# Every second scan step takes its product with B from ScalarE and a transpose on TensorE, not from VectorE or GpSimd

## The chip, the cores and the metric

The kernel runs on one core of one Trainium2 chip. The metric is the device time of one execution in microseconds. Five engines work side by side, each through its own instructions in order: TensorE (PE, with its weight loads as PEld), VectorE (DVE), ScalarE (ACT), GpSimd (POOL) and SyncE (SP), which here only starts DMAs. Semaphores order the engines among each other.

## The reference, cut to what matters

The reference adds four blocks one after the other to an image batch of 8 x 32 x 32 x 64: a diffusion stage, a 3x3 convolution, a Mamba block and a two-dimensional DCT, each behind a group norm. The change is in the Mamba block's selective scan. Per image there are L = 1024 pixels in sequence, 128 inner channels and 16 states:

```python
def step(h, inp):
    u_t, d_t, B_t, C_t = inp
    dA = jnp.exp(d_t[..., None] * A)
    h = dA * h + (d_t * u_t)[..., None] * B_t[:, None, :]
    y = jnp.einsum('bdn,bn->bd', h, C_t)
    return (h, y)
...
return ys.transpose(1, 0, 2) + u * D
```

Here `d_t * u_t` is delta*u. It depends on channel and pixel; B and C depend on state and pixel, and are the same for all channels.

## The kernel before, in words

The 8 images are four pairs, and two pairs make a half; the kernel goes through all stages for half 0 and then for half 1 (`h`). A half has four images `j` in its scan phase, and a scan step `s` of 0 to 63 is one state of one image: `j = s // 16`, state `s % 16`. The layout in the scan is 128 channels on the partitions and 1024 pixels along the free dimension, so the scan over the pixels is one VectorE instruction.

One step needs, in this order:

- ScalarE, `decay` (L881): exp(delta * A) into the buffer `DA[s % 2]`. It waits for scan `s - 2`.
- The product delta*u*B. In three of four steps TensorE copies the row of B to all partitions by two bf16 matmuls with a selecting matrix (`b_rows`, L530; the row is kept as three bf16 parts that add up) into `PS[s % 2]` in PSUM, after scan `s - 2`, and VectorE multiplies it by delta*u in place (L1410). In every fourth step (`s % 4 == 3`, `by_pool`) a DMA copies the row from DRAM to all partitions (`b_row`, L243) and GpSimd multiplies (`input_times_b`, L321) into `DBP`; `decay` then writes its result to `PS[s % 2]`.
- VectorE, `scan_step` (L1403): the scan instruction (L1416) into `HS[s % 2]`. It waits for the decay, the product, and GpSimd's product of step `s - 2`, which reads the same `HS`.
- GpSimd, `state_times_c` (L314): the states times the row of C (L319), which a DMA has brought to all partitions (`c_row`, four buffers in turn), into `HC[s % 2]`. It waits for TensorE's sum of step `s - 2`.
- TensorE, `sum_of` (L538): adds that product to `PS[3]`, by matmuls with the identity; in the first step of an image the product with D is added too (L549). After an image's 16 steps VectorE's `gate` (L1418) reads the sum.

TensorE's order is written out in its loop (L689 to L736): in turn `s` first the broadcast for step `s + 2`, then the sum of step `s - 1`, and behind them the jobs of other stages: the next half's `x_channels` and `group_mean`, and, for the pair finished first, `skip`, `out_proj`, the norm, the last projection and the two DCTs (`xn2_channels` to `second_dct`). ScalarE's loop (L1085) has the decay of step `s` and behind it the copies and sums that belong to these jobs (`keep_x_sums`, `ln_of`, `last_scale`, `x3_sums`, `scale` and others). GpSimd's loop is at L405, VectorE's at L1534, and the queue of SP at L276. In all of them an instruction that waits holds up all behind it.

B and C come out of a projection in the 96 + 32 rows of a PSUM tile; ScalarE keeps the fp32 rows (`keep_rows`, L891) in unused partitions of `BCS32` and `R1`, from where `store_rows` (L226) brings them to DRAM for the row DMAs.

## Time and profile before

| | us |
|---|---|
| median of three runs | 1072.91 |
| lowest, highest | 1071.75, 1073.18 |
| the profiled execution's own time | 1076.65 |
| its span, first to last instruction | 1074.6 |

Busy time over the span: TensorE 824.9 us (77%), VectorE 871.7 (81%), ScalarE 440.2 (41%), GpSimd 656.0 (61%). Busy time does not count waits, and a matmul's duration contains the time in which it drains while the next one already runs; so starts of instructions that follow each other are closer than their durations say. The mean granted TensorE clock was 0.902 of the full 2.4 GHz. The scan phases are from about 276 to 510 us and from about 787 to 1019 us of the span.

### The profile page before, as it was taken

How to read it: one execution, taken by the hardware profiler on the slowest of the kernel's cores; microseconds unless marked ns; L12 is line 12 of the kernel's file. 1: busy time of each engine (PE TensorE's matmuls, PEld its weight loads, DVE VectorE, ACT ScalarE, POOL GpSimd, SP SyncE). 2: the span in 40 equal slices, each digit the busy share in tenths (PEclk: the TensorE clock that was granted, in tenths of full speed). 3: DMA queues.
4: the chain of work that ended last, by engine and by line, in shares of the span. 5: the costliest groups of instructions: out<-in, count | busy, mean ns of one | idle time of the engine just before them, and what ended most of it. 6: DMA issues, size and time to landing. Idle time of an engine off the chain costs nothing.

```text
span 1074.6 us, 6964 instructions
## 1 busy us (share of the span) xinstructions
PE 824.9 (77%) x2210; PEld 379.4 (35%) x2210; DVE 871.7 (81%) x672; ACT 440.2 (41%) x501; POOL 656.0 (61%) x294
## 2 busy tenths in 40 slices
PE   3977998976387877789885999897637787778835
PEld 2433443432133423244443444343213242334414
DVE  5999885479988999999897488547998899999830
ACT  3734331158545333455364423214843423345212
POOL 2446993111699797888361499311169979889810
PEclk8987999988689999999997999998968899999966
DMA  3000000003445564555000100000224555555401
GB/s 96 1 0 0 0 0 1 0 5 107 103 147 192 179 207 176 178 184 167 1 0 3 17 0 0 1 0 5 93 79 138 194 190 195 182 191 193 145 0 20
DMA packets 37808, 91.05 MB, mean 85 GB/s; under 512 B 16264, under 2 KB 16400, under 8 KB 37776
## 3 DMA queue, kind: packets, MB, share of 16 engines
q1 hardware_dynamic: 37456, 89.62, 25.2%
q0 software_dynamic: 320, 1.05, 0.4%
q8 instruction: 15, 0.25, 0.1%
q14 instruction: 17, 0.14, 0.1%
HBM read 87.51 MB, written 3.15 MB: 84 GB/s over the span
## 4 chain that ended last, share of the span: by engine, by line
DVE 39%; PE 32%; POOL 14%; issue 9%; ACT 5%; DMA 1%; SPq 0%; POOLq 0%; DVEq 0%; ACTq 0%
DVE arena L1416 10%; POOL arena L319 9%; PE ps L650 9%; PE ps L446 7%; DVE ps L1410 5%; PE ps L545 4%; ACT arena L754 4%; DVE arena L1371 3%; PE ps L644 3%; DVE arena L1273 3%; POOL arena L327 2%; PE ps L452 2%; POOL arena L312 1%; PE ps L591 1%; PE ps L435 1%
## 5 line engine op out<-in xcount | busy, mean ns | idle before, releaser
L319 POOL TENSOR_TENSOR arena<-arena 128x1024 f32<-128x1024 f32 x128 | 302.5, 2376 | 66.9 <-DVE arena L1416 40.1
L545 PE MATMUL ps<-arena,mat 128*128 128x512 f32 x512 | 270.2, 654 | 69.4 <-POOL arena L319 58.0
L1416 DVE TENSOR_TENSOR_SCAN arena<-arena,ps 128x1024 f32<-128x1024 f32 x96 | 219.5, 2287 | 20.1 <-POOL arena L319 17.2
L754 ACT ACTIVATE arena<-arena,Amat 128x1024 f32<-128x1024 f32 x96 | 109.9, 1148 | 170.6 <-DVE arena L1416 149.3
L545 PEld LDWEIGHTS ps<-arena,mat 128*128 128x128 f32 x512 | 100.6, 205 | 185.0 <-POOL arena L319 98.3
L754 ACT ACTIVATE arena<-arena 128x1024 f32<-128x1024 f32 (+4 forms) x124 | 80.7, 689 | 134.8 <-DVE arena L1339 74.8
L1410 DVE TENSOR_TENSOR ps<-arena,ps 128x1024 f32<-128x1024 f32 x96 | 116.2, 1210 | 4.8 <-PE ps L535 2.7
L650 PE MATMUL ps<-arena,mat 128*128 128x512 f32 x240 | 106.3, 592 | 0.0
L535 PE MATMUL ps<-arena,sel 96*128 96x512 bf16 x192 | 62.2, 409 | 54.5 <-DVE arena L1416 54.1
L446 PE MATMUL ps<-arena,diag 128*128 128x512 f32 x192 | 87.3, 614 | 2.1 <-ACT arena L754 2.1
L327 POOL TENSOR_TENSOR arena<-arena,BB 128x1024 f32<-128x1024 f32 x32 | 75.3, 2354 | 0.0
L754 ACT ACTIVATE arena<-ps 128x1024 f32<-128x1024 f32 (+2 forms) x52 | 52.8, 1017 | 54.2 <-DVE ps L1230 17.0
L1416 DVE TENSOR_TENSOR_SCAN arena<-ps,arena 128x1024 f32<-128x1024 f32 x32 | 72.8, 2276 | 0.2
L446 PE MATMUL ps<-arena,convw 128*128 128x512 f32 x144 | 67.0, 622 | 6.7 <-ACT arena L754 6.7
L650 PEld LDWEIGHTS ps<-arena,mat 128*128 128x128 f32 x240 | 45.6, 190 | 57.4 <-issue 57.4
L342 POOL TENSOR_TENSOR arena<-arena 128x1024 f32<-128x1024 f32 x8 | 24.8, 3108 | 65.7 <-DMA out<-arena 28.1
L754 ACT ACTIVATE ps<-arena,Amat 128x1024 f32<-128x1024 f32 x32 | 35.8, 1118 | 69.9 <-DVE arena L1416 65.2
L302 POOL TENSOR_TENSOR dr<-dv,cpow 128x16 f32<-128x16 f32 x8 | 23.9, 2986 | 58.0 <-DVE dv L1238 43.2
L298 POOL TENSOR_TENSOR dgn<-dgn,cpow 128x1 f32<-128x1 f32 x12 | 7.3, 610 | 83.7 <-DVE dgn L1197 66.7
L308 POOL TENSOR_TENSOR arena<-arena 128x1024 f32<-128x1024 f32 x8 | 21.6, 2704 | 60.0 <-DVE arena L1396 60.0
L535 PEld LDWEIGHTS ps<-arena,sel 96*128 96x128 bf16 x192 | 15.8, 103 | 115.6 <-DVE arena L1416 99.4
L446 PEld LDWEIGHTS ps<-arena,diag 128*128 128x128 f32 x192 | 37.4, 197 | 48.6 <-issue 46.4
(167 smaller groups left out, 1331.5 us busy)
## 6 DMA issues: line engine op xcount, KB each, us to landing
arena<-bc_rows SPq DMA_DIRECT2D x128, 512.0 KB, 4.1
BB<-bc_rows SPq DMA_DIRECT2D x32, 512.0 KB, 4.9
out<-arena SPq DMA_DIRECT2D x32, 64.0 KB, 2.2
xres<-x POOLq DMA_DIRECT2D x4, 256.0 KB, 5.2
bc_rows<-arena SPq DMA_DIRECT2D x8, 128.0 KB, 2.0
xres<-x SPq DMA_DIRECT2D x4, 256.0 KB, 4.4
convw<-conv_w SPq DMA_DIRECT2D x1, 576.0 KB
mat<-mats SPq DMA_DIRECT2D x1, 448.0 KB, 3.5
```

What stands on the lines that cost most here:

```text
L319: tt(HC[s % 2], HS[s % 2], CB[s % 4], ALU.mult).then_inc(S("hc"), 1)
L327: tt(DBP, two_images(s // D_STATE, "DU"), BB, ALU.mult).then_inc(S("dbp"), 1)
L446: last = mm(half(ps, n), taps(tap), frame[:, dy + HB * n:dy + HB * n + HB, dx:dx + W], start=(tap == first), stop=(tap == 8))
L535: last = mm(half(PS[s % 2], n), blk(sel, s % D_STATE), half(two_images(s // D_STATE, "BCS"), n)[0:96, :], start=True, stop=True)
L545: last = mm(half(PS[3], n), ident, half(HC[s % 2], n), start=first, stop=True, skip_group_check=True)
L644: last = mm(half(mix, n), ident, half(a["g"], n), start=False, stop=False, skip_group_check=True)
L650: last = mm(half(mix, n), mt(mname), half(a[src], n), start=False, stop=(name == "e"), skip_group_check=True)
L754: return nc.scalar.activation(out_, in_, func, bias=bias, scale=scale, accum_out=accum_out)
L1273: stt(t, frm(A[k]["fz"])[:, 0:H, tap:tap + W], vecs[:, col:col + 1], t, ALU.mult, ALU.add).then_inc(S("a_tap"), 1)
L1371: stt(d["XI"][:, t:L], PS[2 * k][:, 0:L - t], w[3 - t], d["XI"][:, t:L], ALU.mult, ALU.add)\
L1410: tt(PS[q][:, :], two_images(j, "DU"), PS[q][:, :], ALU.mult).then_inc(S("dbu"), 1)
L1416: nc.vector.tensor_tensor_scan(HS[q], a, b, 0.0, ALU.mult, ALU.add).then_inc(S("scan"), 1)
```

## The change

From step 9 on, every odd step (`X_STEPS`, 28 of a half) makes its product with B another way. Delta*u of the image, 128 channels by 1024 pixels, is turned once by TensorE into eight blocks with 128 pixels on the partitions (`turn_du`), and ScalarE keeps the turned blocks (`keep_du`). The 128 rows of B and C of the four images, now together in the tile `ROWS`, are turned once too (`turn_rows`), and ScalarE keeps B of it (`keep_b`). In this layout B of one state and block is one number per partition. So for step `s` ScalarE makes eight activations of 128x128, each a block times its scale (`scaled_input`, three steps ahead, two buffers `TB`), and TensorE turns the eight results back into `PS[s % 2]` (`turn_scaled`). VectorE scans this directly. All other steps (`Z_STEPS`, 36 of a half: 0 to 8 and the even ones) are made as three of four were before: broadcast by TensorE, product by VectorE. GpSimd's products with B, the row DMAs for them and the buffers `BB` and `DBP` go; `decay` always writes to `DA`.

The turned images pass through `PS[2]`, so TensorE's other jobs that use it are placed anew: `x_channels` and `group_mean` of the next half two turns later each, `skip(0)` from turn 21 to 32, `out_proj(0)` from 22 to 33. ScalarE's and GpSimd's parts of the next half's first norm move by two turns with them. Left out below: three semaphores of the setup and of the norms that are merged with others, and the call of `b_row` ahead of the loop.

```diff
@@ -112,9 +112,10 @@
             d = D[k]
-            d["BCS32"] = d["BCS"]
             d["BCS"] = d["BCS"].bitcast(bf16)
+            d["HI32"] = d["HI"]
             d["HI"] = d["HI"].bitcast(bf16)
+            d["END"] = arena[:, sum(n for _, n in later):][:, 0:BANK]
...
@@ -129,7 +130,9 @@
         DA, HS = [[D[0][f"W{2 * m + q}"] for q in range(2)] for m in (0, 2)]
-        DBP, BB = D[0]["R1"], sb("BB", L)[:, :]
+        ROWS = sb("ROWS", L)[:, :]
+        TB = [ROWS, D[1]["R1"]]
+        BT = D[0]["HI32"].rearrange("p (k j n) -> p k j n", k=BLK, n=D_STATE)
         CB = [D[0]["W2"], D[0]["W3"], D[1]["W0"], D[1]["W1"]]
...
@@ -153,16 +156,21 @@
         SCANS = 4 * D_STATE
-        BY_POOL = SCANS // 4
-
-        def by_pool(s):
-            return s % 4 == 3
-
-        def row_fill(s):
-            return s - s // 4 + 1
+        X_STEPS = [s for s in range(9, SCANS, 2)]
+        Z_STEPS = [s for s in range(SCANS) if s not in X_STEPS]
         def rows_f32(j):
-            return D[j // 2]["R1" if j % 2 else "BCS32"][96:128, :]
+            return ROWS[32 * j:32 * j + 32, :]
+
+        def du_block(j, n):
+            if j % 2 == 0:
+                return blk(D[1]["W4"], n)
+            return blk(D[n // 4]["END"], n % 4)
+
+        def turned(h, j):
+            return 5 * h + [1, 3, 4, 5][j]
+
+        ROWS_TURNED = 2
...
@@ -240,14 +248,6 @@
-            def b_row(h, s):
-                j = s // D_STATE
-                if s % D_STATE < 4:
-                    sp.wait_ge(S(f"rows{j % 2}"), 32 * h + 16 * (j // 2 + 1))
-                if s >= 4:
-                    sp.wait_ge(S("dbp"), BY_POOL * h + s // 4)
-                load_row(BB, j, s % D_STATE, "b_row")
-
             def store_out(h, k):
...
@@ -275,8 +274,6 @@
                     c_row(h, s)
-                    if s % 4 == 0:
-                        b_row(h, s + 3)
                     if s == SCANS - 3:
...
@@ -317,14 +314,6 @@
                 tt(HC[s % 2], HS[s % 2], CB[s % 4], ALU.mult).then_inc(S("hc"), 1)
-
-            def input_times_b(h, s):
-                pool.wait_ge(S("b_row"), 16 * (BY_POOL * h + s // 4 + 1))
-                if s % D_STATE == 3 and s > 3:
-                    pool.wait_ge(S("du"), 4 * h + s // D_STATE + 1)
-                if s >= 4:
-                    pool.wait_ge(S("scan"), SCANS * h + s - 3)
-                tt(DBP, two_images(s // D_STATE, "DU"), BB, ALU.mult).then_inc(S("dbp"), 1)
...
@@ -396,21 +385,13 @@
                 delta_u(h, 1)
-                pool.wait_ge(S("r10"), 2 * h + 2)
-                pool.wait_ge(S("bcs0"), ONE + 2 * h + 2)
-                plain(pool)
-                pool.wait_ge(S("rows1"), 32 * h + 16)
-                pool.wait_ge(S("du"), 4 * h + 1)
-                input_times_b(h, 3)
                 for s in range(SCANS):
                     state_times_c(h, s)
-                    if by_pool(s) and s + 4 < SCANS:
-                        input_times_b(h, s + 4)
                     if s == 5:
                         delta_u(h, 2 + s // 16)
-                    if h + 1 < HALVES and s in (13, 21):
+                    if h + 1 < HALVES and s in (15, 23):
                         root(A[s // 16], h + 1, 0, s // 16)
...
@@ -528,12 +509,31 @@
             def b_rows(h, s):
-                if s < SCANS and not by_pool(s):
-                    if s >= 2:
-                        pe.wait_ge(S("scan"), SCANS * h + s - 1)
-                    for n in range(2):
-                        last = mm(half(PS[s % 2], n), blk(sel, s % D_STATE), half(two_images(s // D_STATE, "BCS"), n)[0:96, :], start=True, stop=True)
-                    last.then_inc(S("bb"), 1)
+                if s >= 2:
+                    pe.wait_ge(S("scan"), SCANS * h + s - 1)
+                for n in range(2):
+                    last = mm(half(PS[s % 2], n), blk(sel, s % D_STATE), half(two_images(s // D_STATE, "BCS"), n)[0:96, :], start=True, stop=True)
+                last.then_inc(S("bb"), 1)
+
+            def turn_scaled(h, s):
+                i = X_STEPS.index(s)
+                pe.wait_ge(S("scaled"), len(X_STEPS) * h + i + 1)
+                pe.wait_ge(S("scan"), SCANS * h + s - 1)
+                transposes(TB[i % 2], PS[s % 2]).then_inc(S("bb"), 1)
+
+            def fill(h, s):
+                if s in Z_STEPS:
+                    b_rows(h, s)
+                if s in X_STEPS:
+                    turn_scaled(h, s)
+
+            def turn_du(h, j):
+                pe.wait_ge(S("du"), 4 * h + j + 1)
+                transposes(two_images(j, "DU"), PS[2]).then_inc(S("turned"), 1)
+
+            def turn_rows(h):
+                pe.wait_ge(S("kept"), turned(h, 0))
+                transposes(ROWS, PS[2]).then_inc(S("turned"), 1)
...
@@ -690,28 +690,41 @@
                         plain(pe)
-                    b_rows(h, s + 2)
+                    fill(h, s + 2)
                     sum_of(h, s - 1)
+                    if s == 2:
+                        pe.wait_ge(S("rx1"), 2 * h + 2)
+                        turn_du(h, 0)
+                    if s == 3:
+                        turn_rows(h)
+                    if s == 5:
+                        pe.wait_ge(S("kept"), 5 * h + ROWS_TURNED)
+                        turn_du(h, 1)
+                    if s == 23:
+                        if h + 1 < HALVES:
+                            pe.wait_ge(S("group1"), g_var(h + 1, 0))
+                        else:
+                            pe.wait_ge(S("kept"), turned(h, 1))
+                        turn_du(h, 2)
+                    if s == 28:
+                        pe.wait_ge(S("kept"), turned(h, 2))
+                        turn_du(h, 3)
+                    if s == 32:
+                        pe.wait_ge(S("kept"), turned(h, 3))
+                        skip(0)
                     if h + 1 < HALVES:
-                        if s == 5:
-                            pe.wait_ge(S("rx1"), 2 * h + 2)
+                        if s == 7:
+                            pe.wait_ge(S("kept"), turned(h, 1))
                             x_channels(h + 1, 0, PS[2])
-                        if s == 10:
+                        if s == 12:
                             group_mean(A[0], h + 1, 0, 0)
-                        if s == 13:
+                        if s == 15:
                             pe.wait_ge(S("a_x"), 2 * h + 3)
                             x_channels(h + 1, 1, PS[2])
-                        if s == 18:
+                        if s == 20:
                             group_mean(A[1], h + 1, 0, 1)
-                        if s == 21:
-                            pe.wait_ge(S("a_x"), 2 * h + 4)
-                            pe.wait_ge(S("group1"), g_var(h + 1, 0))
-                            skip(0)
-                    elif s == 21:
-                        pe.wait_ge(S("rx1"), 2 * h + 2)
-                        skip(0)
-                    if s == 22:
+                    if s == 33:
                         out_proj(h, 0)
...
@@ -881,12 +894,47 @@
                     j, q = s // D_STATE, s % 2
-                    act.wait_ge(S("delta"), 4 * h + j + 1)
+                    if s % D_STATE == 0:
+                        act.wait_ge(S("delta"), 4 * h + j + 1)
                     if s >= 2:
                         act.wait_ge(S("scan"), SCANS * h + s - 1)
-                    plain(act)
-                    dst = PS[q][:, :] if by_pool(s) else DA[q]
-                    av(dst, two_images(j, "DL"), ACT.Exp, Amat[:, s % D_STATE:s % D_STATE + 1]).then_inc(S("da"), 1)
+                    if s % D_STATE == 0:
+                        plain(act)
+                    av(DA[q], two_images(j, "DL"), ACT.Exp, Amat[:, s % D_STATE:s % D_STATE + 1]).then_inc(S("da"), 1)
+
+            def keep_du(h, j):
+                act.wait_ge(S("turned"), turned(h, j))
+                if j >= 2:
+                    act.wait_ge(S("scaled"), len(X_STEPS) * h + sum(1 for s in X_STEPS if s < D_STATE * (j - 1)))
+                if j == 0:
+                    act.wait_ge(S("delta"), 4 * h + 3)
+                    av(D[1]["W4"], PS[2][:, :], ACT.Identity).then_inc(S("kept"), 1)
+                elif j == 2:
+                    av(D[1]["W4"], PS[2][:, :], ACT.Identity).then_inc(S("kept"), 1)
+                else:
+                    av(D[0]["END"], half(PS[2], 0), ACT.Identity)
+                    av(D[1]["END"], half(PS[2], 1), ACT.Identity).then_inc(S("kept"), 1)
+
+            def keep_b(h):
+                act.wait_ge(S("turned"), 5 * h + ROWS_TURNED)
+                act.wait_ge(S("bcs0"), ONE + 2 * h + 2)
+                ps = PS[2][:, :].rearrange("p (k j n) -> p k j n", k=BLK, n=2 * D_STATE)
+                av(BT, ps[:, :, :, 0:D_STATE], ACT.Identity).then_inc(S("kept"), 1)
+
+            def scaled_input(h, s):
+                i, j = X_STEPS.index(s), s // D_STATE
+                if i == 0:
+                    for r in range(2):
+                        act.wait_ge(S(f"rows{r}"), 32 * h + 32)
+                if i == 1:
+                    act.wait_ge(S("bcs1"), ONE + 4 * h + 4)
+                if i > 1:
+                    act.wait_ge(S("bb"), SCANS * h + X_STEPS[i - 2] + 1)
+                if i == 0 or X_STEPS[i - 1] // D_STATE < j:
+                    act.wait_ge(S("kept"), turned(h, j) if i else 5 * h + ROWS_TURNED)
+                for n in range(BLK):
+                    last = av(blk(TB[i % 2], n), du_block(j, n), ACT.Identity, BT[:, n, j, s % D_STATE:s % D_STATE + 1])
+                last.then_inc(S("scaled"), 1)
...
@@ -1086,15 +1134,26 @@
                         hi_rows(h, 1)
+                        keep_du(h, 0)
+                    if s == 5:
+                        keep_b(h)
+                    if s + 3 in X_STEPS:
+                        scaled_input(h, s + 3)
+                    if s == 7:
+                        keep_du(h, 1)
+                    if s == 25:
+                        keep_du(h, 2)
+                    if s == 30:
+                        keep_du(h, 3)
                     if s == D_STATE - 1:
                     if h + 1 < HALVES:
-                        if s in (8, 16):
-                            keep_x_sums(h + 1, s // 16)
-                        if s in (12, 20):
-                            small_group_var(A[s // 16], h + 1, 0, s // 16)
-                        if s in (15, 23):
-                            small_group_shift(A[s // 16], h + 1, 0, s // 16)
+                        if s in (10, 18):
+                            keep_x_sums(h + 1, s // 18)
+                        if s in (14, 22):
+                            small_group_var(A[s // 18], h + 1, 0, s // 18)
+                        if s in (17, 25):
+                            small_group_shift(A[s // 18], h + 1, 0, s // 18)
                     if s == 38:
...
@@ -1402,18 +1461,14 @@
                 j, q = s // D_STATE, s % 2
-                if by_pool(s):
-                    dve.wait_ge(S("dbp"), BY_POOL * h + s // 4 + 1)
-                    a, b = PS[q][:, :], DBP
-                else:
-                    dve.wait_ge(S("bb"), (SCANS - BY_POOL) * h + row_fill(s))
+                dve.wait_ge(S("bb"), SCANS * h + s + 1)
+                if s in Z_STEPS:
                     tt(PS[q][:, :], two_images(j, "DU"), PS[q][:, :], ALU.mult).then_inc(S("dbu"), 1)
-                    dve.wait_ge(S("dbu"), (SCANS - BY_POOL) * h + row_fill(s))
-                    a, b = DA[q], PS[q][:, :]
+                    dve.wait_ge(S("dbu"), len(Z_STEPS) * h + Z_STEPS.index(s) + 1)
                 dve.wait_ge(S("da"), SCANS * h + s + 1)
                     dve.wait_ge(S("hc"), SCANS * h + s - 1)
-                nc.vector.tensor_tensor_scan(HS[q], a, b, 0.0, ALU.mult, ALU.add).then_inc(S("scan"), 1)
+                nc.vector.tensor_tensor_scan(HS[q], DA[q], PS[q][:, :], 0.0, ALU.mult, ALU.add).then_inc(S("scan"), 1)
                 dve.wait_ge(S("sum"), SCANS * h + D_STATE * (j + 1))
...
```

## Rows read from the trace of the kernel before

**Rows 1.** The page's busy time: engine, us (share of the span), instructions.
```profile
PE 824.9 (77%) x2210; PEld 379.4 (35%) x2210; DVE 871.7 (81%) x672; ACT 440.2 (41%) x501; POOL 656.0 (61%) x294
```
**Rows 2.** Groups of instructions by form: busy us, mean ns of one | idle before, releasers.
```profile
L319 POOL TENSOR_TENSOR arena<-arena 128x1024 f32<-128x1024 f32 x128 | 302.5, 2376 | 66.9 <-DVE arena L1416 40.1 <-PE ps L545 25.6 <-DMA arena<-bc_rows 0.7
...
L1416 DVE TENSOR_TENSOR_SCAN arena<-arena,ps 128x1024 f32<-128x1024 f32 x96 | 219.5, 2287 | 20.1 <-POOL arena L319 17.2
L1410 DVE TENSOR_TENSOR ps<-arena,ps 128x1024 f32<-128x1024 f32 x96 | 116.2, 1210 | 4.8 <-PE ps L535 2.7 <-POOL arena L312 2.1
L754 ACT ACTIVATE arena<-arena,Amat 128x1024 f32<-128x1024 f32 x96 | 109.9, 1148 | 170.6 <-DVE arena L1416 149.3 <-issue 20.6 <-ACT xres L754 0.4
...
L327 POOL TENSOR_TENSOR arena<-arena,BB 128x1024 f32<-128x1024 f32 x32 | 75.3, 2354 | 0.0
...
L754 ACT ACTIVATE arena<-arena 128x1024 f32<-128x1024 f32 x56 | 57.0, 1050 | 55.5 <-DVE arena L1263 19.7 <-DVE arena L1288 11.1 <-DVE arena L1396 8.3
...
L754 ACT ACT_TABLE_LOAD x23 | 29.5, 1283 | 2.2 <-issue 1.1 <-PEq L1627 0.7
```
**Rows 3.** VectorE's waits, 275 to 511 us: us in total, times, longest.
```profile
DVE arena L1416 <- POOL arena L319: 9.7, 11, 1.5
DVE ps L1410 <- PE ps L535: 1.8, 4, 0.8
```
**Rows 4.** Timeline, VectorE: start us, length us, engine, line, operation.
```profile
354.40 2.26 DVE L1416 TENSOR_TENSOR_SCAN arena<-ps,arena 128x1024 f32<-128x1024 f32 x1
356.58 1.21 DVE L1410 TENSOR_TENSOR ps<-arena,ps 128x1024 f32<-128x1024 f32 x1
357.82 2.29 DVE L1416 TENSOR_TENSOR_SCAN arena<-arena,ps 128x1024 f32<-128x1024 f32 x1
360.03 1.21 DVE L1410 TENSOR_TENSOR ps<-arena,ps 128x1024 f32<-128x1024 f32 x1
```
**Rows 5.** Timeline, VectorE: the scans of steps 7 and 63, first half.
```profile
308.71 2.29 DVE L1416 TENSOR_TENSOR_SCAN arena<-ps,arena 128x1024 f32<-128x1024 f32 x1
...
507.82 2.29 DVE L1416 TENSOR_TENSOR_SCAN arena<-ps,arena 128x1024 f32<-128x1024 f32 x1
```
**Rows 6.** Groups by form and timeline, ScalarE: a short copy, two long activations.
```profile
L754 ACT ACTIVATE dtw<-ps 128x128 f32<-128x128 f32 x1 | 0.3, 278 | 7.9 <-PE ps L429 7.9
...
504.71 2.37 ACT L754 ACTIVATE arena<-xres,agn 128x1024 f32<-128x1024 f32 x2
```
**Rows 7.** Timeline, TensorE: sum, eight transposes, broadcast, sum, without a gap.
```profile
977.65 1.88 PE L545 MATMUL ps<-arena,mat 128*128 128x512 f32 x4
979.37 1.04 PE L435 MATMUL ps<-mat,arena 128*128 128x128 f32 x8
980.24 0.60 PE L535 MATMUL ps<-arena,sel 96*128 96x512 bf16 x2
980.68 1.88 PE L545 MATMUL ps<-arena,mat 128*128 128x512 f32 x4
```
**Rows 8.** Timeline, TensorE: two jobs of the last stage, one behind the other.
```profile
492.41 1.95 PE L591 MATMUL ps<-mat,arena 128*128 128x128 f32 x16
494.19 1.88 PE L596 MATMUL ps<-arena,mat 128*128 128x512 f32 x4
```
**Rows 9.** Timeline, SP's queue: the last store of B and C rows, first half.
```profile
278.91 0.32 SPq L230 DMA_DIRECT2D bc_rows<-arena  x1
```
**Rows 10.** Stretches: PE, PEld, DVE, ACT, POOL busy, clock, DMA; one timeline row.
```profile
800.00:850.00 50.00, 37.03 (x72) 13.88 (x71) 44.68 (x27) 18.00 (x16) 39.36 (x17) 0.81 0.47 158
...
296.00:300.00 4.00, 4.00 (x7) 1.52 (x6) 3.96 (x3) 1.99 (x2) 1.75 (x2) 0.50 0.37 125
...
295.52 3.62 PE L545 MATMUL ps<-arena,mat 128*128 128x512 f32 x4
...
450.00:500.00 50.00, 41.10 (x140) 20.13 (x140) 48.14 (x27) 24.29 (x29) 42.23 (x20) 1.00 0.56 192
```

19 lines of the change are left out of this document (9 added, 10 removed).

## Prediction

> **What bounds the kernel now.** I read the page's busy times, then the groups of instructions, then VectorE's waits inside the two scan phases, and at last short stretches of the timeline. VectorE is the busiest engine [rows 1]; its largest groups are the scans of L1416 (2.287 us) and the products of L1410 (1.210 us) [rows 2]. In the first half's scan phase VectorE waits only 9.7 us for GpSimd's product with C and 1.8 us for TensorE's broadcast [rows 3]; over both halves it is 17.2 and 2.7 us [rows 2]. The rest is its own work, so the scan phase is bound by VectorE, with GpSimd close behind: per four steps GpSimd makes four products with C and one with B, 5 x 2.31 = 11.6 us (starts follow each other some 0.05 us closer than the durations of [rows 2]).
>
> The timeline gives the pitches that count. From the product to its scan 1.24 us, from a scan to the next product 2.20 us, a scan that follows a scan directly costs 2.18 to 2.20 us [rows 4]. Four steps before: 3 x 1.24 + 4 x 2.20 = 12.5 us. From the end of step 7's scan (308.71 + 2.29 = 311.0) to that of step 63 (510.1) the first half takes 199.1 us for 56 steps [rows 5], which holds 175 us of that pattern, 11 us of waits and, as the rest, 13 us of gates, norms and one delta that VectorE does between the steps.
>
> **What is removed.** L1410's product ran in 48 of 64 steps of a half (three of four); now it runs in 36, the 28 odd steps from 9 have none. Steps 3 and 7, which GpSimd served, now have one; that is in the count. So 12 fewer per half, 24 x 1.24 = 29.8 us, all on the path, since VectorE is what the others wait for. GpSimd's 32 products of 2.354 us go. Its demand per pair of steps falls to 4.6 us while VectorE's pair is 1.24 + 2 x 2.20 = 5.65 us, so the waits for L319, 17.2 us, go too; the 2.7 us behind L535 I drop here and count anew below. The B rows' 32 DMAs go from SP's queue, ahead of C rows that were not late; nothing for that. Sum so far: 49.7 us.
>
> **What is added on ScalarE.** Per pair of steps eight activations of 128x128 with a scale per partition. The trace has none. The nearest row is the 128x128 copy of dtw, 0.278 us [rows 6], without a scale operand; such an operand costs about 1.148 - 1.050 = 0.10 us in the long forms [rows 2], and two long activations in a row take 2.37 us where each has 1.23 [rows 6], so they overlap by 0.1. Bounds: 0.18 us each (the copy, overlapped) to 0.38 us (copy and operand, no overlap); I take 0.28 to 0.29, the copy and operand with the overlap, 2.3 to 2.4 us per eight. The Trainium skill, ScalarE: Activation LUTs, What ACT_TABLE_LOAD costs, gives 186 ns + 0.833 ns per element, 93 ns per pointer operand and 93 ns of overlap, which would be 0.29 us each.
>
> ScalarE's pair is two decays at 1.06 us and the eight: 4.5 us of 5.65 (4.2 to 5.2 by the bounds). Place matters: the eight stand between decay(s) and decay(s+1), s even. Call T the end of scan s-2. Decay(s) starts at T+0.1, the eight end at T+3.6, decay(s+1) at T+4.7. Scan s+1 wants it at T+5.65: 0.95 us to spare. Whatever else stands in an even turn is late by what exceeds that. keep_x_sums (steps 10 and 18, first half) and x3_sums (step 48) hold two full activations, 2.1 us: 1.2 us late each. ln_of(3) in step 15 needs two table loads of 1.28 us [rows 2] around it, 3.5 us: the next two decays come 1.4 us late in all. The small ones (variance, last_scale, square) 0.5 us. Together 5.5 us in the first half, 3.1 in the second. The copies of the turned delta*u in odd turns have the slack of a whole pair and cost nothing; the early ones (steps 4 to 7) fall where no scaled input is made yet.
>
> **What is added on TensorE.** A turned X step replaces a broadcast of 0.44 us by eight transposes, which in a row with others take 980.24 - 979.37 = 0.87 us; a sum_of is 1.72 us [rows 7]. Pair: 2 x 1.72 + 0.44 + 0.87 = 4.75 us of 5.65, at 2.4 GHz. In order: after T the broadcast for s and sum(s-3) until T+2.3; at T+2.3 scan s-1 is over and the transposes for s+1 go, done at T+3.4, wanted at T+5.65. sum(s-2) ends at T+5.1, just before GpSimd wants its buffer. So a lone extra job of 1.7 us is absorbed, and a pair recovers 0.9 us. Between steps 8 and 63 there are, in the first half, about 12 jobs of 1.72 to 1.78 us, one of them in [rows 8], and 6 sets of transposes: 26 us against 28 x 0.9 = 25 us of room and VectorE's 13 us of other work. What overflows is where they cluster. skip(0) and out_proj(0) move from steps 21 and 22 to 32 and 33, beside the diagD product behind gate(1) and out_proj(1): four jobs, 7 us, in three steps; their waits leave a broadcast 1.7 us late. At 57 to 60 keep_x3, second_dct, skip(1) and out_proj(2) are 7 us in under two pairs: 7 - 1.7 - 1.3 = 4 us. So 5.7 us per half.
>
> The rest is priced at nothing: C rows have four buffers; the last store of the B and C rows, for which the first scaled input waits, is issued at 278.9 us [rows 9], seven steps earlier; GpSimd's roots move two steps with the jobs they serve. After a scan phase the same chain of products, sums and gate follows.
>
> **Sum.** 29.8 + 17.2 + 2.7 - 5.5 - 3.1 - 11.4 = 29.7 us. The profiled execution took 1076.65 us (span 1074.6 and 2.05 around it), 3.74 over the median shown. Its own time becomes 1047.0; as I see no reason for the scatter to change, the median becomes 1072.91 - 29.7 = 1043.2 us. Ends: with ScalarE's low bound and stalls that hide behind VectorE's other work (5 us left in all) the gain is 44.7, 1028.2 us; with 0.38 us per block the spare 0.95 us is nearly gone and some eight late decays per half cost 0.7 more each, 11 us: 1054.4 us.
>
> **Rivals.**
> 1. *The late jobs hide (1029 us).* For it: VectorE's 13 us of other work per half fall partly on the same steps (norms at 36 to 40, add_block at 46). Against: steps 57 to 60 have none.
> 2. *ScalarE becomes the bound (1056 us).* If a block costs 0.4 us or more the pair is 2.1 + 3.2 = 5.3 us, and with 24 us of other activations per half (estimated from the listed jobs) 6.2 us per pair, what VectorE needs with its own (5.65 + 13/28 = 6.1). It decides from 0.4 us on; the copy's row speaks against.
> 3. *TensorE becomes the bound and the kernel is slower (1100 us).* TensorE's work of a half after step 8 is 28 x 4.75 + 26 = 159 us at full clock, against 199.1 us now. It equals that when the mean granted clock is 0.80. In 800 to 850 us it was 0.81, and at the lower level a sum_of takes 3.62 us [rows 10]. At 0.75 the half takes 212 us, 13 us more than before, twice: about 1100 us. Against it: the falls of the clock in the scan phase follow stretches in which TensorE sat waiting for GpSimd or VectorE, and its longest regular gap is now 0.9 us; from 450 to 500 us, when it was busiest, 1.00 was granted [rows 10]. The Trainium skill, TensorE: Matmul & The Clock Gate, Part 4: PE-mode transpose, says that transposes don't count as busy for the clock. By it 3.9 of 5.65 us would still count, a greater share than now, so it would move only this rival's chance.
> 4. *No change (1072 us).* The X step's chain (ScalarE, TensorE, scan) could hold VectorE back 1 us per pair, eating the gain: 56 pairs x 0.9 = 50 us. The three steps of lead and two buffers speak against.
>
> **Chances.** Forecast (its own range 1036 to 1052) 0.62; rival 1 0.12; rival 2 0.13; rival 3 0.08; rival 4 0.05. The 80% range is 1026 to 1060 and leaves out mostly rivals 3 and 4. A difference of 0.2%, about 2 us, is what can be told here. Faster 0.88, same 0.03, slower 0.09 (rival 3 and a part of 4).
>
> **What would show it.** Right: 72 products of L1410's kind on VectorE in place of 96, each still 1.21 us; 128 scans of 2.29 us; waits of the scan for GpSimd nearly gone, new ones of some 20 us in all behind ScalarE's activations (first half steps 11, 19, 49) and TensorE (around steps 36 and 60); the new 128x128 activations at 0.37 to 0.39 us of duration and 0.29 us apart; a set of transposes 0.87 us apart from what follows; a granted clock of 0.95 or more in both scan phases. Wrong: scans that wait for transposes or decays in every pair (rivals 2, 4), granted clock under 0.85 from 320 us on (rival 3), or GpSimd still named ahead of the scans.

## The result, and the profile after

The kernel after took 1055.3 us, the median of four runs (1054.6 to 1057.35); the kernel before, in four runs beside it, 1073.03 us (1071.75 to 1073.18). The ratio is 0.9833, with a 95% interval of 0.9811 to 0.9856: 17.7 us faster, where 29.7 us were forecast. The time lies inside the forecast's 80% range (1026 to 1060 us), but outside its own range of 1036 to 1052 us. The profiled execution took 1057.35 us, 2.05 us over the median, with a span of 1055.5 us (before: 1074.6).

First the busy time of the page, to be held against [rows 1], and the shares of the chain that ended last:

```profile
PE 848.6 (80%) x2690; PEld 424.4 (40%) x2690; DVE 839.5 (80%) x648; ACT 574.0 (54%) x963; POOL 585.1 (55%) x262
...
PE 42%; DVE 37%; ACT 8%; POOL 6%; issue 6%; DMA 0%; DVEq 0%; SPq 0%; POOLq 0%; ACTq 0%
```

VectorE has 32 us less to do, GpSimd 71 us less, ScalarE 134 us more and TensorE 24 us more. Work has moved from the busiest engine to the one with the most room. But VectorE lost 32 us and the kernel only 17.7, so the waits grew. The groups by form say behind whom (busy us, mean ns of one | idle before, releasers; before: [rows 2]):

```profile
L316 POOL TENSOR_TENSOR arena<-arena 128x1024 f32<-128x1024 f32 x128 | 304.3, 2384 | 113.9 <-DVE arena L1471 62.3 <-PE ps L545 49.6
L1471 DVE TENSOR_TENSOR_SCAN arena<-arena,ps 128x1024 f32<-128x1024 f32 x128 | 289.5, 2280 | 18.5 <-POOL arena L316 9.2 <-ACT arena L767 4.9 <-PE ps L416 1.6
...
L1466 DVE TENSOR_TENSOR ps<-arena,ps 128x1024 f32<-128x1024 f32 x72 | 87.1, 1210 | 7.7 <-PE ps L515 5.7 <-POOL arena L309 2.1
...
L767 ACT ACTIVATE ROWS<-arena 128x128 f32<-128x128 f32 x224 | 68.2, 389 | 0.0
```

L316 is what L319 was, L1471 the scan (L1416), L1466 the product (L1410), L515 the broadcast (L535). There are 72 products, still 1.210 us each, and 128 scans. The scans' wait for GpSimd has fallen only from 17.2 to 9.2 us. The new names in the list are the decay (ACT L767, 4.9 us), the transposes (PE L416, 1.6 us), and more of the broadcast (5.7 for 2.7 us). GpSimd, which has no product with B any more, now waits 49.6 us for TensorE's sums (before 25.6) and 62.3 us for scans (before 40.1): it is held up, not busy.

The two scan phases, from the first scan to the last, as stretches (us, then PE, PEld, DVE, ACT, POOL busy, clock, DMA share, GB/s), after and then before:

```profile
277.60:497.00 219.40, 188.31 (x760) 102.56 (x761) 204.01 (x114) 168.93 (x347) 161.85 (x72) 0.96 0.47 152
779.40:998.30 218.90, 188.39 (x740) 100.87 (x741) 203.93 (x113) 157.66 (x321) 160.81 (x70) 0.95 0.44 147
```

```profile
277.00:510.00 233.00, 178.50 (x522) 80.62 (x522) 219.54 (x125) 102.16 (x116) 198.59 (x88) 0.91 0.54 177
788.60:1018.60 230.00, 176.91 (x502) 77.93 (x502) 219.75 (x125) 90.77 (x90) 197.47 (x86) 0.91 0.51 174
```

VectorE is busy 15.5 and 15.8 us less, as 12 products of 1.24 us per half had to give. Its idle time is the difference of first and third column: before 13.5 and 10.3 us, after 15.4 and 15.0 us, so 6.6 us more in all. The granted clock was 0.91 before and is 0.96 and 0.95 after. Where the idle time lies, the list of VectorE's waits tells, for 275 to 505 us (us in total, times, longest; before: [rows 3]):

```profile
DVE arena L1471 <- ACT arena L767: 4.2, 4, 1.4
DVE arena L1471 <- POOL arena L316: 2.9, 4, 1.2
DVE ps L1466 <- PE ps L515: 2.8, 2, 1.4
DVE ps L1289 <- ACT dm L767: 2.5, 1, 2.5
```

The last row is one wait in each half, 2.54 us long where it was 0.28 before, that nothing in the forecast had. L1289 takes the mean from each image column in the last norm (`center`); ScalarE makes the mean (`small_mean`, step 38).

From here on the measure is the scan phases: the time from the start of the first scan to the end of the last, both halves added, read from the timeline of the profiled run of each kernel. Outside them the same code takes up to some us more or less from one run to the next (the stretch between the phases 282.3 us in the first profiled run of the kernel after, 279.9 us in the second), so small differences in whole times are not read there. The scan phases scatter too. The kernel after had 438.4 and 439.8 us. The kernel before was profiled once, in an execution 3.74 us over its median; e5 below, the same kernel with two jobs moved, agrees with it in the second half (229.9 and 230.1 us) and is 3.8 us shorter in the first (229.3 and 233.1), where it was granted 0.95 of the clock and not 0.91. So of the 24.8 us that the phases shrank, up to 4 may belong to that one execution of before.

| kernel | scan phases, us | all else, us | median, us | ratio to before (95%) |
|---|---|---|---|---|
| before | 463.2 | 611.4 | 1073.0 | |
| after | 438.4 | 617.2 | 1055.3 | 0.9833 (0.9811 to 0.9856) |
| after_again | 439.8 | 613.8 | 1055.1 | 0.9805 (0.9771 to 0.9838) |
| e10_all_broadcast | 479.7 | 611.3 | 1092.1 | 1.0151 (1.0127 to 1.0176) |
| e2_every_fourth | 454.1 | 613.3 | 1069.4 | 0.9942 (0.9922 to 0.9962) |
| e5_before_moved | 459.2 | 609.5 | 1072.2 | 0.9975 (0.9953 to 0.9997) |
| e3_one_scale | 430.3 | 617.0 | 1048.9 | 0.9759 (0.9723 to 0.9795) |
| e4_no_turn_back | 434.4 | 613.3 | 1049.3 | 0.9759 (0.9721 to 0.9796) |
| e1_mean_first | 433.8 | 612.4 | 1048.9 | 0.9764 (0.9725 to 0.9803) |
| e6_tail_spread | 436.1 | 618.8 | 1055.9 | 0.9814 (0.9781 to 0.9848) |
| e7_spread_all | 427.5 | 617.2 | 1046.7 | 0.9738 (0.9704 to 0.9771) |
| e8_tail_again | 426.7 | 615.6 | 1046.6 | 0.9739 (0.9718 to 0.9760) |
| e9_pool_job_later | 425.7 | 618.8 | 1047.1 | 0.9739 (0.9719 to 0.9759) |

The ratios are to the kernel before on the same chip. Its median is 1073.0 us beside the first run of the kernel after, and 1075.4 to 1075.9 us beside all others, so medians are compared by the ratio.

### The profile page after: what moved, and what is told of

Same layout as the page of the kernel before. It is cut to its first block, busy times and chain, and to the rows that moved or that the text cites. A ratio compares the mean times of both kernels' runs of the same rounds, so it can differ in the third digit from the quotient of the medians.

```text
span 1055.5 us, 8217 instructions
## 1 busy us (share of the span) xinstructions
PE 848.6 (80%) x2690; PEld 424.4 (40%) x2690; DVE 839.5 (80%) x648; ACT 574.0 (54%) x963; POOL 585.1 (55%) x262
## 3 DMA queue, kind: packets, MB, share of 16 engines
q0 software_dynamic: 320, 1.05, 0.4%
## 4 chain that ended last, share of the span: by engine, by line
PE 42%; DVE 37%; ACT 8%; POOL 6%; issue 6%; DMA 0%; DVEq 0%; SPq 0%; POOLq 0%; ACTq 0%
DVE arena L1471 11%; PE ps L650 9%; PE ps L427 8%; PE ps L545 8%; ACT arena L767 6%; DVE ps L1466 4%; PE ps L433 3%; PE ps L644 3%; POOL arena L316 3%; PE ps L416 3%; DVE arena L1430 3%; DVE arena L1332 3%; PE ps L515 1%; DVE arena L1460 1%; PE ps L591 1%
## 5 line engine op out<-in xcount | busy, mean ns | idle before, releaser
L316 POOL TENSOR_TENSOR arena<-arena 128x1024 f32<-128x1024 f32 x128 | 304.3, 2384 | 113.9 <-DVE arena L1471 62.3
L1471 DVE TENSOR_TENSOR_SCAN arena<-arena,ps 128x1024 f32<-128x1024 f32 x128 | 289.5, 2280 | 18.5 <-POOL arena L316 9.2
L545 PE MATMUL ps<-arena,mat 128*128 128x512 f32 x512 | 251.6, 616 | 8.8 <-POOL arena L316 7.9
L767 ACT ACTIVATE arena<-arena 128x128 f32<-128x128 f32 (+4 forms) x348 | 148.7, 495 | 129.5 <-DVE arena L1398 74.8
L767 ACT ACTIVATE arena<-arena,Amat 128x1024 f32<-128x1024 f32 x128 | 146.1, 1144 | 90.0 <-DVE arena L1471 86.4
L545 PEld LDWEIGHTS ps<-arena,mat 128*128 128x128 f32 x512 | 95.8, 197 | 91.1 <-issue 68.8
L650 PE MATMUL ps<-arena,mat 128*128 128x512 f32 x240 | 106.3, 592 | 0.0
L1466 DVE TENSOR_TENSOR ps<-arena,ps 128x1024 f32<-128x1024 f32 x72 | 87.1, 1210 | 7.7 <-PE ps L515 5.7
L515 PE MATMUL ps<-arena,sel 96*128 96x512 bf16 x144 | 45.7, 403 | 52.4 <-DVE arena L1471 52.4
L767 ACT ACTIVATE arena<-ps 128x1024 f32<-128x1024 f32 (+2 forms) x58 | 54.1, 942 | 61.7 <-DVE ps L1289 17.0
L416 PE MATMUL ps<-mat,arena 128*128 128x128 f32 x448 | 61.1, 282 | 29.4 <-DVE arena L1302 16.8
L416 PEld LDWEIGHTS ps<-mat,arena 128*128 128x128 f32 x448 | 52.9, 146 | 55.7 <-issue 30.7
L650 PEld LDWEIGHTS ps<-arena,mat 128*128 128x128 f32 x240 | 45.6, 190 | 57.4 <-issue 57.4
L767 ACT ACTIVATE ROWS<-arena 128x128 f32<-128x128 f32 x224 | 68.2, 389 | 0.0
L515 PEld LDWEIGHTS ps<-arena,sel 96*128 96x128 bf16 x144 | 11.1, 99 | 96.2 <-DVE arena L1471 78.5
```

Of the source, the lines that this page charges most:

```text
L316: tt(HC[s % 2], HS[s % 2], CB[s % 4], ALU.mult).then_inc(S("hc"), 1)
L416: last = nc.tensor.transpose(blk(dst, n), blk(src, n), ident)
L515: last = mm(half(PS[s % 2], n), blk(sel, s % D_STATE), half(two_images(s // D_STATE, "BCS"), n)[0:96, :], start=True, stop=True)
L545: last = mm(half(PS[3], n), ident, half(HC[s % 2], n), start=first, stop=True, skip_group_check=True)
L650: last = mm(half(mix, n), mt(mname), half(a[src], n), start=False, stop=(name == "e"), skip_group_check=True)
L767: return nc.scalar.activation(out_, in_, func, bias=bias, scale=scale, accum_out=accum_out)
```

## The experiments

### The wait for the mean

```diff
                         keep_b(h)
+                    if s == 38:
+                        small_mean(h, 0)
                     if s + 3 in X_STEPS:
                         scaled_input(h, s + 3)
...
                     if s == 38:
-                        small_mean(h, 0)
                         square(h, 0, 1)
```

> The changed kernel with one move in ScalarE's turn 38: the small mean of the norm, for which VectorE waits in the middle of its centring, goes ahead of the eight scaled blocks of step 41 and no longer behind them. Theory (places in the queues are what costs): VectorE's wait of 2.54 us there falls to 0.3 us in each half, 4.5 us in all, 1055.3 to about 1051 us. Rival (the amount of work on ScalarE and TensorE costs, the order does not): the wait turns up again at the next scan, time within 1 us of the changed kernel.

Timeline of the kernel after, around step 38:

```profile
405.54 1.21 DVE L1282 TENSOR_REDUCE dm<-ps 128x16 f32<-128x1024 f32 x1
...
406.71 2.43 ACT L767 ACTIVATE ROWS<-arena 128x128 f32<-128x128 f32 x8
...
409.05 0.20 ACT L767 ACTIVATE dm<-dm 128x16 f32<-128x16 f32 x1
409.28 1.23 DVE L1289 TENSOR_TENSOR ps<-ps,dm 128x1024 f32<-128x1024 f32 x1 [2.54 <-ACT dm L767]
```

The activation that VectorE wants takes 0.20 us, but it is queued behind the eight scalings. With it ahead of them, in the first half:

```profile
406.84 1.23 DVE L1290 TENSOR_TENSOR ps<-ps,dm 128x1024 f32<-128x1024 f32 x1 [0.28 <-ACT dm L767]
```

2.54 - 0.28 = 2.26 us, twice 4.5 us; the scan phases fell from 438.4 to 433.8 us, 4.5 us. The wait goes where it was said to go, and does not turn up again at the next scans: the theory was right. That the two sums agree to the tenth is more than a scatter of 1.5 us between two runs of one kernel lets one read. The median fell by 6.4 us (on another chip), more than the phases; I read only the 4.5.

### Half the steps, and none

```diff
-        X_STEPS = [s for s in range(9, SCANS, 2)]
+        X_STEPS = [s for s in range(9, SCANS, 4)]
```

> The changed kernel with the new form in every fourth step from 9 (14 steps of a half in place of 28); the others take the broadcast and VectorE's product. VectorE gets 28 more products of 1.24 us, 34.7 us. Theory: half the load of the new form, but the clusters of other jobs stay, so some 8 to 10 of the 30 us of waits in the scan phases go: 1080 to 1083 us. Rival (every new step costs a wait of its own): 15 us of waits go, 1075 us. If no wait depends on the share of new steps: 1090 us.

```diff
-        X_STEPS = [s for s in range(9, SCANS, 2)]
+        X_STEPS = []
```

> The changed kernel with no step in the new form: all 64 take the broadcast and VectorE's product, GpSimd makes none. VectorE has 56 more products of 1.24 us than in the changed kernel, 69.4 us. Theory (the waits come of the load of the new form beside the other jobs): the waits of the scan phases fall from 30 us to about 6, so 1055 + 69 - 24 = 1100 us, and a new step in the changed kernel is worth 0.8 us on average, more in the first 28 (every fourth) than in the last 28. Rival (the waits come with GpSimd and TensorE's sums, whatever form the steps have): 15 us or more of waits stay, 1110 us.

The first half's scan phase of the kernel with every fourth step, and of the one with none:

```profile
276.70:503.58 226.88, 187.20 (x678) 95.72 (x678) 220.38 (x128) 138.35 (x235) 163.24 (x72) 0.94 0.45 147
```

```profile
276.90:517.05 240.15, 184.48 (x594) 86.27 (x594) 237.04 (x142) 107.69 (x123) 163.49 (x72) 0.94 0.42 139
```

With none VectorE is idle for 240.15 - 237.04 = 3.1 us. The first 14 steps of a half make it busy 16.7 us less and idle 3.4 us more, the next 14 make it busy 16.4 us less and idle 8.9 us more (219.4 - 204.0 = 15.4). Over both halves the first 28 steps bring 479.7 - 454.1 = 25.5 us, 0.91 each, and the next 28 bring 15.8 us, 0.56 each, of the 1.24 that a product costs. The forecast took the full 1.24 and a list of stalls that don't depend on their number.

Both expectations of e2 were too high (1080 to 1083 and 1075 us for 1069.4): 28 more products are 34.7 us, the scan phases grew by 15.8, so 18.9 us of waits went, and neither theory had more than 15. With a pair of steps more between two sets of scalings nearly every wait goes but the one for the mean (its waits from 275 to 510 us):

```profile
DVE ps L1289 <- ACT dm L767: 2.5, 1, 2.5
DVE ps L1466 <- POOL arena L309: 1.0, 1, 1.0
DVE arena L1475 <- PE ps L545: 0.8, 3, 0.4
DVE arena L1471 <- POOL arena L316: 0.5, 2, 0.4
```

The run with none also splits the change in two. It keeps the moved jobs and the turned images, so the parts are these. GpSimd's products with B given back to VectorE, with those two, cost 16.5 us (479.7 - 463.2): 32 more products are 39.7 us, and most of the 23.8 us of idle time goes (3.1 and 2.6 us are left in the halves, where there were 13.5 and 10.3). The path over ScalarE and TensorE then gives 41.3 us, 0.74 us per step. The theory's waits were right (about 6 us left of 30) and its time, 1100 us for 1092.1, too high: 5.9 of the 8 us lie outside the scan phases (611.3 for 617.2 us).

### ScalarE's scalings, and the way back through TensorE

The first kernel has one activation of 1024 elements (two of 512 for odd images) in place of eight; it leaves out the scale of each block and applies one for all.

```diff
-                for n in range(BLK):
-                    last = av(blk(TB[i % 2], n), du_block(j, n), ACT.Identity, BT[:, n, j, s % D_STATE:s % D_STATE + 1])
+                if j % 2 == 0:
+                    last = av(TB[i % 2], D[1]["W4"], ACT.Identity, BT[:, 0, j, s % D_STATE:s % D_STATE + 1])
...
```

> The changed kernel with each scaled input made by one activation of 128x1024 (odd images: two of 128x512) with one scale, not by eight of 128x128; the values are not those of the reference. ScalarE loses about 1.3 us per new step, 70 us of busy time. Theory: only the waits that name ScalarE go, 4.9 us of scans and 4 to 5 us of the centring: about 1046 us, and the waits for TensorE and GpSimd stay as they are. Rival (ScalarE's rate bounds the pair of steps): 15 us or more, 1040 us.

The scan phases are 8.1 us shorter: the decays' stalls went with the shorter queue (scans' wait for ScalarE 4.9 to 0.4 us), the wait for the mean fell from 2.54 to 1.24 us in each half, as the one activation still stands ahead of it, and GpSimd's stayed. The theory (about 9 us, only waits that name ScalarE) was right, the rival's 15 us were not there:

```profile
L1474 DVE TENSOR_TENSOR_SCAN arena<-arena,ps 128x1024 f32<-128x1024 f32 x128 | 288.8, 2279 | 13.2 <-POOL arena L316 8.8 <-PE ps L416 1.6 <-ACT arena L767 0.4
```

The second kernel leaves out the eight transposes back; a broadcast stands in their place, so VectorE scans other values.

```diff
-                transposes(TB[i % 2], PS[s % 2]).then_inc(S("bb"), 1)
+                for n in range(2):
+                    last = mm(half(PS[s % 2], n), blk(sel, s % D_STATE), ...)
+                last.then_inc(S("bb"), 1)
```

> The changed kernel with the eight transposes of a new step replaced by the two bf16 matmuls of the broadcast (0.44 in place of 0.87 us of TensorE's queue); the scaled blocks are still made and waited for but not used, so the values are not those of the reference. Theory: TensorE's clusters of jobs overflow less: of its waits (about 7 us named for TensorE, and the part of the 9.2 us for GpSimd in which GpSimd waited for a sum) about 9 us go, 1046 us. Rival (GpSimd's own extra jobs make the remaining waits for it, and TensorE has room): 3 us, 1052 us.

It gave 3.9 us and not 9, nearer to the rival's 3. Its reason holds for GpSimd too: the scans' waits for it fell from 9.2 to 5.5 us, and all that are left stand at steps 13, 28 and 41, behind jobs of GpSimd's own. But TensorE has no room where its jobs are close together. At step 36 the broadcast is still late without the transposes' length:

```profile
401.29 1.23 DVE L1468 TENSOR_TENSOR ps<-arena,ps 128x1024 f32<-128x1024 f32 x1 [0.96 <-PE ps L515]
```

From step 60 on, the waits of 1.43, 0.79 and 0.79 us are 0.82, 0.79 and 0.16 us. So ScalarE's longer queue costs about 8 us and the transposes' length about 4 us, the latter hardly more than the 1.5 us of scatter allow to tell; the granted clock was a little lower in this run (0.93 in both phases).

### Jobs moved in the kernel before

```diff
-                            skip(0)
                     elif s == 21:
                         pe.wait_ge(S("rx1"), 2 * h + 2)
+                    if s == 32:
                         skip(0)
-                    if s == 22:
+                    if s == 33:
                         out_proj(h, 0)
```

> The kernel before with one part of the change alone: skip(0) goes from TensorE's turn 21 to 32 and out_proj(0) from 22 to 33, beside the product with D and out_proj(1). Theory (the cluster of four jobs is what makes the broadcast of step 36 late): VectorE waits 1 to 1.7 us there in each half, the scan phases get 2 to 3 us longer. Rival (only the transposes' load makes it late; in the kernel before TensorE has room): within 0.5 us of before.

In the kernel before, the move costs nothing (scan phases 459.2 against 463.2 us; of these 4 us 3.8 lie in the first half, beside a higher clock, see above), though it makes the same cluster of four jobs. The broadcast in question:

```profile
407.43 1.23 DVE L1410 TENSOR_TENSOR ps<-arena,ps 128x1024 f32<-128x1024 f32 x1 [0.38 <-PE ps L535]
```

After the change the same place has 1.40 us:

```profile
402.07 1.23 DVE L1466 TENSOR_TENSOR ps<-arena,ps 128x1024 f32<-128x1024 f32 x1 [1.40 <-PE ps L515]
```

So the cluster hurts only together with the rest of the change. The rival's time was right, but not its reason that only the transposes' load makes the broadcast late: in e4, with a broadcast in their place, 0.96 of the 1.40 us stayed. That the rest comes from VectorE's shorter pair (5.65 us, where two steps took 12.5 / 2 = 6.3 us) is what is left, and no run tests it by itself.

### Another order for the same work

e6 spreads the last stage's jobs on TensorE over steps 57 to 62, e7 does this and puts the jobs of steps 33 to 46 and `keep_x_sums` one turn later, so that ScalarE's part of them stands in turns in which it has no scalings. The kernel after was run and profiled once more beside them.

```diff
+                    if s == 58:
                         second_dct(h, 0)
-                    if s == 60:
+                    if s == 61:
                         pe.wait_ge(S("ot"), 2 * h + 1)
                         skip(1)
+                    if s == 62:
                         out_proj(h, 2)
```

> The changed kernel with TensorE's last jobs spread: second_dct from turn 57 to 58, skip(1) from 60 to 61, out_proj(2) from 60 to 62. Theory: the waits of 1.43 us (step 60), 0.79 and 0.79 us (61 and 63) go in each half and the last gate waits 5 us and not 6.3: 6 to 8 us in all, 1048 us where the changed kernel has 1055. Rival (TensorE is over its limit there however its jobs are placed): the waits move to steps 61 to 63, 2 us or less.

```diff
-                    if s == 33:
+                    if s == 34:
                         out_proj(h, 0)
-                    if s == 34:
+                    if s == 35:
                         out_proj(h, 1)
...
-                        if s in (10, 18):
-                            keep_x_sums(h + 1, s // 18)
+                        if s in (11, 19):
+                            keep_x_sums(h + 1, s // 19)
...
-                    if s == 38:
+                    if s == 39:
                         small_mean(h, 0)
```

> As the one before, and out_proj(0) and out_proj(1) a turn later (34, 35), the norm of the first pair a step later (centring after step 37, so that ScalarE's small mean stands in an odd turn, where no scaled blocks are), GpSimd's root, the last projection and add_block with it, and keep_x_sums in the odd turns 11 and 19. The work is the same. Theory (places): of the 30 us of waits in the two scan phases about 18 go: dm 4.5, step 36 2.8, keep_x_sums 1.9, the root 2.4, the end 6 to 7; about 1038 us, below both kernels. Rival (the amounts of work on ScalarE and TensorE set the waits): 1050 us.

> The changed kernel once more, unaltered, so that the next three are held against it on one chip. The phases outside the scans differed by up to 3 us between runs of kernels that are alike there; both theories expect the two scan phases at 219.5 and 218.9 us again, within 0.3, and a ratio to before of 0.983.

The repeated kernel agrees with the first within 0.2 us in the median and 1.5 us in the scan phases. e6 brought 3.7 us of the scan phases (439.8 to 436.1) and nothing of the median (1055.9 us), where the theory had 6 to 8 us. In the kernel after a broadcast was 1.43 us late near step 60 (timeline row 483.92). With the jobs spread that wait is gone, and one behind ScalarE's `copy_out` has its place:

```profile
488.22 2.29 DVE L1473 TENSOR_TENSOR_SCAN arena<-arena,ps 128x1024 f32<-128x1024 f32 x1 [1.84 <-ACT arena L769]
```

and behind the second half's phase the last gate waits 7.58 instead of 6.29 us for its sum. e7 shows what the order is worth where it can be mended: 12.3 us of the scan phases (439.8 to 427.5) of the 18 that the theory had, and 8.4 us of the median; its rival had 1050 us, so 1046.7 us lies between the two, and what the order cannot mend stays. (e7 is the spread of e6 and the turns moved together; the step from e6 to e7 is 8.6 us of the phases.) The broadcasts (L515, in e7 numbered otherwise) are not waited for at all, the mean 0.3 us a half. Its list for 275 to 498 us:

```profile
DVE arena L1473 <- ACT arena L769: 3.6, 4, 1.8
DVE arena L1473 <- POOL arena L316: 2.5, 3, 1.6
...
DVE ps L1291 <- ACT dm L769: 0.3, 1, 0.3
```

Two more tries took what was left. e8 is e7 with `skip(1)` back at step 60 and `copy_out` at 61; e9 is e8 with GpSimd's `delta_u(2)` at step 17 instead of 10.

```diff
-                    if s == 60:
+                    if s == 61:
                         copy_out(h, 0)
```

> As the kernel with all jobs spread, but the end of the half ordered anew: ScalarE's copy of the finished image goes from turn 60 to 61 (behind the decay of step 61, which had waited 1.85 us behind it), skip(1) back to turn 60, out_proj(2) stays at 62. Theory (a job may stand only where no awaited instruction is queued behind it, on ScalarE as on TensorE): the wait of 1.85 us at step 61 goes in both halves, and the last gate waits about 1 us less: 5 us less in all, 1042 us. Rival (the end is bound by TensorE's amount of work): the wait comes back as one for TensorE, within 1 us of 1047.

```diff
-                    if s in (10, 25):
-                        delta_u(h, 2 + s // 16)
+                    if s == 17:
+                        delta_u(h, 2)
+                    if s == 25:
+                        delta_u(h, 3)
```

> As the one before, and GpSimd's product delta*u of the third image goes from its turn 10 to turn 17, where VectorE has a gate and a delta between the scans. Theory: the wait of 1.57 us for GpSimd at step 13 is that job standing ahead of a product with C; it goes in both halves: 3 us less than the one before. Rival (the product with C is late for TensorE's sums): no change.

Both took away the wait they were made for and got another in exchange, so both theories missed (1042 us for 1046.6, and 3 us less for none in the median; the scan phases fell by 0.8 and 1.0 us, less than can be told). The rival of e8, within 1 us of 1047 and another wait in place of the one removed, was right. In e8 the 1.84 us went and these came:

```profile
481.29 2.29 DVE L1473 TENSOR_TENSOR_SCAN arena<-arena,ps 128x1024 f32<-128x1024 f32 x1 [0.62 <-PE ps L416]
...
485.60 2.29 DVE L1473 TENSOR_TENSOR_SCAN arena<-arena,ps 128x1024 f32<-128x1024 f32 x1 [0.90 <-POOL arena L316]
```

In e9 the wait for GpSimd at step 13 (1.57 us, below) went in both halves, which shows GpSimd's job there as its cause. Without it the decay that follows the table loads of `ln_of` is 1.06 us late in the first half, which that wait had covered in e8, and the first half's last gate waits 4.34 us for its sum, where it waited 0.93 in e8:

```profile
335.94 2.29 DVE L1475 TENSOR_TENSOR_SCAN arena<-arena,ps 128x1024 f32<-128x1024 f32 x1 [1.06 <-ACT arena L771]
...
500.05 1.23 DVE L1479 TENSOR_TENSOR arena<-ps,arena 128x1024 f32<-128x1024 f32 x1 [4.34 <-PE ps L547]
```

e7, e8 and e9 all beat both kernels and can't be told apart; 0.974 of before is the best found.

## Why the prediction was right, and where its size was off

The sign, the engine and the mechanism held; the gain was 17.7 us for 29.7. Of the profiled executions' 19.1 us of span, the scan phases gave 24.8 (23.3 with the second run of the kernel after), and the rest of the kernel took 5.7 back. Term by term, with the profiled executions:

| term | forecast, us | measured, us |
|---|---|---|
| products off VectorE | -29.8 | -31.4 |
| scans' waits for GpSimd | -17.2 | -8.0 |
| TensorE: waits of before, new stalls | -2.7 + 11.4 | -2.7 + 7.3 |
| late decays | +8.6 | +4.9 |
| wait for the mean | 0 | +4.5 |
| sum in the scan phases | -29.7 | -25.4 (read from the timeline: -24.8) |
| outside them | 0 | +5.7; second run +2.3 |

That the sum for the scan phases came within 5 us is in part luck. Two terms promised 13.7 us too much (GpSimd's waits 9.2, the mean 4.5), and three promised 9.4 too little (TensorE 4.1, decays 3.7, products 1.6). The sums of the forecast come out as written, but for one bound: with 0.18 us per block ScalarE's pair is 2.1 + 1.4 = 3.6 us and not 4.2; no term hangs on it.

**The products.** Right: VectorE's busy time in the phases fell by 15.5 and 15.8 us.

**GpSimd's waits all go.** This step failed (the text named it as the sign: GpSimd still ahead of the scans), and it is the largest error: 9.2 of 17.2 us stayed (the same 17.2 us are 13.6 in e5). Its argument was a balance over a pair, 4.6 us of GpSimd in 5.65 of VectorE, and the balance is true: GpSimd sat waiting for 113.9 us in `state_times_c`. But a job of GpSimd's own between two products takes 2.35 us at once, and the room of a pair is 5.65 - 4.6 = 1.05. At step 13 of the second half:

```profile
824.78 2.35 POOL L309 TENSOR_TENSOR arena<-arena 128x1024 f32<-128x1024 f32 x1
...
827.10 4.65 POOL L316 TENSOR_TENSOR arena<-arena 128x1024 f32<-128x1024 f32 x2
...
829.57 2.29 DVE L1471 TENSOR_TENSOR_SCAN arena<-arena,ps 128x1024 f32<-128x1024 f32 x1 [1.57 <-POOL arena L316]
```

`delta_u` (L309) pushes the two products back and the scan with them; the last norm's root (2.91 us at 419.94) does the same, 1.19 us at 425.29 and again in the second half; behind the next image's `delta_u` it is 0.30 and 0.49 us. These are 4.7 of the 9.2 us. No job on GpSimd is named in the forecast, though such jobs are for the other two engines. The other 4.5 us stand behind TensorE, whose late sums hold GpSimd (49.6 us of waits, most of them hidden): near step 60, at step 43, and once at step 21, after a fall of the clock. There TensorE had been without work for 2.11 us, then a sum ran at the lower clock (0.50 granted from 852 to 854 us), 3.42 us where it is 1.88 at the full one, and 1.12 us reached the scan:

```profile
850.67 0.80 PE L515 MATMUL ps<-arena,sel 96*128 96x512 bf16 x2 [2.11 <-DVE arena L1471]
...
851.26 3.42 PE L545 MATMUL ps<-arena,mat 128*128 128x512 f32 x4
...
857.35 2.29 DVE L1471 TENSOR_TENSOR_SCAN arena<-arena,ps 128x1024 f32<-128x1024 f32 x1 [1.12 <-POOL arena L316]
```

**ScalarE.** The price was right: eight scalings are 2.43 us, the last one lasting 0.39, so they start 2.04 / 7 = 0.29 us apart. (The formula of the Trainium skill, ScalarE: Activation LUTs, What ACT_TABLE_LOAD costs, agrees: it gives 0.29 us of pitch, and 389 ns of duration were measured for its 386.) In the first half stalls stand where they were put, at step 11 (1.40 us for 1.2) and, by `ln_of`, at 16 and 17 (1.21 and 1.09 us, for 1.4 in all). Three small ones have 0.29 to 0.48 us. In the second half `ln_of` costs 0.41 us for 1.4, as GpSimd's wait at step 13 covers it: in e9, without that wait, it is 0.56 and 1.09 us. The stalls of steps 19 and 49, at 1.2 us each, are not there. VectorE has a long job of its own just ahead (2.49 us at 344.77 ahead of step 18, 2.01 us at 442.42 ahead of step 47); that this is the cover rival 1 spoke of fits, but no run tests it.

**What stood behind ScalarE's eight.** The missed term. The forecast asked what the eight do to the decay and not to the other activations of an even turn for which somebody waits at once. `small_mean` is 0.20 us long and stood behind 2.43 us; e1 shows it.

**TensorE.** The two places are right: 1.40 us at step 36 (forecast 1.7), and from step 60 on 1.43 and twice 0.79 us, 3.0 in all (forecast 4). In the table one 0.79 of each half is counted with GpSimd, whose name it bears. e5 shows that moved jobs alone cost nothing, e4 that these four waits fall from 4.4 to 2.7 us a half without the transposes' length.

**After the phases.** Priced at nothing, and not quite nothing: TensorE's queue is longer at step 63, so the last gate of the second half waits 6.29 us for its sum where it waited 4.97. This is 1.3 us. Of the other 4.4 us, 3.4 are the difference of two runs of the same kernel (617.2 and 613.8). Some of it may be real: all ten profiled runs with new steps have 612.4 to 618.8 us outside the phases, the two of the old form and e10 609.5 to 611.4. Its cause stays open.

**Rivals.** 2 gave 1056 us, nearest to the measured time, but for a reason that the trace denies: a scaling does not take 0.4 us, and no row of waits runs through every pair. What is true of it is that the new step's worth falls as ScalarE and TensorE fill (0.91, then 0.56 us). e3 also denies that ScalarE's rate bounds the pair. Rival 3 (clock) did not happen but for single falls; 4 is out; of 1, late decays did hide in part (4.9 of 8.6 us were left), while GpSimd's late jobs, which it did not name, showed.

## What to carry to other kernels

When work moves off the busiest engine, sum the room of the others per period, but then go through every job that stands between two periodic ones on every engine, GpSimd too: if it is longer than the slack of one period it can stall the bound engine, however idle its own engine is on average. Its length less that slack is only a first guess: here it gives 1.3 us for `delta_u`, which cost 0.3 to 1.6, and 1.9 us for the root, which cost 1.2. Ask of each short instruction behind a new long one who waits for it at once, and put it ahead; that was worth 4.5 us here for three lines. Expect the first units moved to bring more than the last, and try half of the change: here the second half of the steps brought 0.56 us each, the first 0.91.

## What the runs showed of the hardware

- No run shows a loss of granted clock by the transposes. In the first scan phase the clock was 0.96 and 0.94 in the two runs with 28 sets of eight, 0.94 with 14 sets, 0.94 with none and 0.93 in e4, where 28 broadcasts replace them, against 0.91 before. (By the Trainium skill, TensorE: Matmul & The Clock Gate, Part 4: PE-mode transpose, they don't count as busy; with 0.9 us of them in 5.65 no run here shows a loss by it.) What raised it from 0.91 stays open: e5, the kernel before with two jobs moved, had 0.95 in the first phase and 0.92 in the second.
- A short wait of TensorE came before a fall of the clock in one place and not in another. After 2.11 us without work at step 21 the sum took 3.42 us, and a wait of 0.8 to 1.1 us stands at this step of the second half in every run with 28 new steps a half. In e2 a gap of 2.05 us (before 856.56) was followed by a sum of 1.88 us.
- The time between the scan phases was 282.3 and 279.9 us in two runs of the same kernel, and 278.4 to 284.7 us over thirteen profiled runs; the scan phases of that kernel agreed to 1.5 us in 440, those of the old form (before and e5) to 4.0. Differences of 4 us are told by places of waits, not by the whole time.
